# Gated product ahead of the scaling of o, and a cross attention that takes its four batches together

## The chip, the core and the metric

The kernel runs on one NeuronCore of a Trainium2 chip. Its engines are TensorE (PE in the rows, PEld for its weight loads), VectorE (DVE), ScalarE (ACT), GpSimd (POOL) and SyncE (SP), which here only issues transfers. Each engine runs its own instructions in the order of the program and waits on semaphores for the others. The metric is device time in microseconds (us), median of the runs; lower is better.

## The reference, cut to what matters

The input x is 4 batches of 512 tokens with 128 channels, the context 4 batches of 77 tokens. A cross attention is added to x through a gate, and then a stack of six layers of windowed attention and feed-forward.

```
xn = layernorm(x);  q = xn @ Wq.T + bq;  k, v = ctx @ Wk.T + bk, ctx @ Wv.T + bv
a  = softmax(q @ k.T / sqrt(128)) @ v
x  = x + tanh(g_xattn) * ((xn + a) @ Wo.T + bo)
y  = layernorm(x)
for i in range(6):                       # 16 heads of 64, windows of 32 tokens that look one window back
    y = attn(shift_tokens(y)) + y        # q and k with l2norm and rotary tables
    y = ffn(shift_tokens(y)) + y         # (a * gelu(gate)) @ W2 + b2, inner width 341
x  = x + tanh(g_ffn) * y
```

All data are float32.

## The kernel before

**The main loop.** The six layers are run as 192 units: a group is one layer of one batch (24 groups), and a group has 8 units (4 blocks of 128 tokens, two halves of the heads). One loop of 214 slots `n` is written out on each engine; `s = n % 8` is the place in the group. In slot n the engines work on several units at once: TensorE makes queries and keys of unit n, the scores of n-3, the product of probabilities and values (`attend`) of n-5, and so on. The feed-forward of group g-2 is spread over the slots by `s`. Its result is built in `uT`: TensorE's `up` products of the gate and of a, ScalarE's `gelu` on the gate, and VectorE's `gated(g, k)` (L942), which multiplies block k of a into it.

**Three PSUM banks in a ring.** Nearly every TensorE product of the loop goes to the next of three banks (`RING`), and waits until the result that stood there three turns ago has been read. In slot s = 3 the last turns are `up("gate", 1)`, `up("a", 0)`, `transpose_q`; in slot s = 4 the first are `attend` (L437), `values` (L378), `transpose_o` (L450). So `values` of s = 4 takes the bank of block 0 of a, and waits for `gated(g - 2, 0)`, which frees it.

**VectorE and GpSimd in a unit.** VectorE scales `o` by the inverse sum (`scale_o`, L884, reads the bank of `attend`), sums the next probabilities (L866), makes the inverse norms by a Newton step of three small instructions on 16 columns (`newton`, L823, L826, L828, two SBUF operands each), and scales k (L836) and q (L844). GpSimd then turns k and q by the rotary tables: L1033, L1040, L1076 for k, L1033, L1040, L1069 for q, all on SBUF.

**The cross attention** comes before the loop, in pairs of batches. The chain of a pair: statistics (L760, L763) on VectorE, inverse root on GpSimd (L1016, L1018), normalise (L769) on VectorE, transpose (L303), queries (L307), scores (L311), softmax on VectorE and ScalarE (L779 to L789, L590), transpose (L317), bias row (L321), attend (L326), transpose (L332), output projection (L337), the gated update of x (L800), again statistics and normalise (L760 to L769), transpose (L344) and copy to `xT` (L600, L601). The second pair uses the buffers and banks of the first, and so starts when the first is through. Ahead of both stand keys and values of the context (L289, L294, L295). GpSimd zeroes `kB` (L1008) first of all and multiplies the rotary tables (L1023) after the last inverse root.

Of the kernel before, what the change touches and what calls it, by code (L numbers as in the profile page):

```python
# [9 lines left out]
ALU = mybir.AluOpType  # L10
# [3 lines left out]
P = 128  # L14
B, N, C = 4, 512, 128
CTX = 77
# [50 lines left out]
def build(nc, x_in, ctx_in, g_xattn, g_ffn, Wq, bq, Wk, bk, Wv, bv, Wo_x, bo, Wqkv, q_scale, k_scale,  # L67
          Wo, ln_g, ln_b, W1, b1, W2, b2, rope_in, mats_in, mask_in, out):
    ctx = ExitStack()
    with ctx:  # L70
# [73 lines left out]
        xn_x = [quad(turned[:, j, 0, :]) for j in range(2)]  # L144
        xnT_x = [turned[:, j, 1, :] for j in range(2)]
        q_x = [turned[:, j, 2, :] for j in range(2)]
        res_x = [quad(turned[:, j, 3, :]) for j in range(2)]
        pr_x = [quad(qkn[:, j, 0:TPG * CTX], CTX) for j in range(2)]
        pT_x = [flat(pT[:, j]) for j in range(2)]
        rT_x = [flat(qT[:, j]) for j in range(2)]  # L150
        x_nat = oT[:, 0:B, :].rearrange("p b (t c) -> p (b t) c", c=C)
        small = lambda j, start, n: sq[:, 64 * j + start:64 * j + start + n]
        stats_x = [quad(small(j, 0, 6 * TPG), 6) for j in range(2)]
        mv_x = [quad(small(j, 24, 2 * TPG), 2) for j in range(2)]
        vare_x, rstd_x, mx_x, rs_x, rr_x = ([small(j, 32 + 4 * i, TPG) for j in range(2)] for i in range(5))
# [120 lines left out]
        def _(pe):  # L276
# [3 lines left out]
            for i in range(4):  # L280
                mm = pe.transpose(ps[0][:, i * C:(i + 1) * C], wx_in[:, i, :], ident[:, :])
            mm.then_inc(wxT_mm, 1)
            for b in range(B):
                mm = pe.transpose(ps[1][:, b * CTX:(b + 1) * CTX], ctx_sb[:, b, :], ident[0:CTX, 0:CTX])
            mm.then_inc(ctxT_mm, 1)
            pe.wait_ge(wxT_ev, 1)
            pe.wait_ge(ctxT_ev, 1)
            pe.wait_ge(cst_ready, 4)
            pe.matmul(ps[2][:, 0:B * CTX], wxT[:, 1, :], ctxT[:, :, :].rearrange("p b s -> p (b s)"),  # L289
                      start=True, stop=True).then_inc(kx_mm, 1)  # L290
# [6 lines left out]
            pe.wait_ge(kx_ev, 1)  # L297
            pe.wait_ge(vx_ev, 1)
            for pair in range(B // 2):
                for j in range(2):  # L300
                    pe.wait_ge(a_xn, 4 * (2 * pair + j) + 4)
                    for t in range(TPG):
                        mm = pe.transpose(ps[4 * j][:, t * P:(t + 1) * P], xn_x[j][:, t, :], ident[:, :])  # L303
                    mm.then_inc(a_xnT, 1)
                for j in range(2):
                    pe.wait_ge(a_xnTev, 2 * pair + j + 1)
                    pe.matmul(ps[4 * j + 1][:, :], wxT[:, 0, :], xnT_x[j], start=True, stop=True).then_inc(a_q, 1)  # L307
                for j in range(2):
                    pe.wait_ge(a_qev, 2 * pair + j + 1)
                    for t in range(TPG):  # L310
                        mm = pe.matmul(ps[4 * j + 2][:, t * P:t * P + CTX], q_x[j][:, t * P:(t + 1) * P],  # L311
                                       kxT[:, 2 * pair + j, :], start=True, stop=True)
                    mm.then_inc(a_sc, 1)
                for j in range(2):
                    pe.wait_ge(a_pn, 2 * pair + j + 1)
                    for t in range(TPG):
                        mm = pe.transpose(ps[4 * j + 3][0:CTX, t * P:(t + 1) * P], pr_x[j][:, t, :], ident[:, :])  # L317
                    mm.then_inc(a_pT, 1)
                for j in range(2):

                    pe.matmul(heads(ps[4 * j + 2][:, :], C), ones[0:1, :],  # L321
                              brow[0:1, 1, :].unsqueeze(1).to_broadcast([1, TPG, C]), start=True, stop=True)
                for j in range(2):
                    pe.wait_ge(a_pTev, 2 * pair + j + 1)
                    for t in range(TPG):
                        mm = pe.matmul(ps[4 * j][:, t * P:(t + 1) * P], pT_x[j][0:CTX, t * P:(t + 1) * P],  # L326
                                       vx[:, 2 * pair + j, :], start=True, stop=True)
                    mm.then_inc(a_att, 1)
                for j in range(2):
                    pe.wait_ge(a_res, 2 * pair + j + 1)  # L330
                    for t in range(TPG):
                        mm = pe.transpose(ps[4 * j + 1][:, t * P:(t + 1) * P], res_x[j][:, t, :], ident[:, :])  # L332
                    mm.then_inc(a_rT, 1)
                for j in range(2):
                    pe.wait_ge(a_rTev, 2 * pair + j + 1)
                    for t in range(TPG):
# [3 lines left out]
                for j in range(2):  # L340
                    b = 2 * pair + j
                    pe.wait_ge(b_x, 4 * b + 4)
                    for t in range(TPG):
                        mm = pe.transpose(ps[4 * j + 1][:, t * P:(t + 1) * P], x_nat[:, TPG * b + t, :], ident[:, :])  # L344
# [892 lines left out]
```

## Time and profile before

| | |
|---|---|
| median of 3 runs | 1879.38 us (1878.95 to 1880.2) |
| profiled execution, its own time | 1880.17 us |
| its span, first to last instruction | 1878.4 us |
| TensorE busy | 1770.3 us, 94% of the span |
| VectorE busy | 1610.7 us, 86% |
| GpSimd busy | 1499.3 us, 80% |
| ScalarE busy | 1326.8 us, 71% |
| cross attention and what is ahead of it | to 85.07 us, the first product of the loop |

A busy share is an average over the whole span, and a waiting instruction does not count as busy. Whether an engine that is busy for most of the time is also the one that sets the time is seen only from what it waited for, and from what the others waited for.

### The profile page before, as it was taken

Reading aid. Unit: us, or ns where it says so; the run is one execution under the profiler, and the core shown is the slowest. Engines: PE = TensorE matmul, PEld = TensorE weight load, DVE = VectorE, ACT = ScalarE, POOL = GpSimd, SP = SyncE. Lnnn points to the kernel's source line nnn. Section 1 sums busy time; section 2 is a strip of 40 time slices with the busy share of each in tenths; the row PEclk is TensorE's granted clock in tenths of the full one; section 3 lists DMA queues with packets and bytes.
Section 4 is the critical chain, followed back from the end, with each engine's and each line's share of the span. In section 5 each row is a group of like instructions: output and inputs, shape, how many; then the busy total and the mean of one; then the engine's idle time right before and its main releaser. Section 6 shows DMA issues by size and latency. Waiting matters only on the chain.

```text
span 1878.4 us, 48610 instructions
## 1 busy us (share of the span) xinstructions
PE 1770.3 (94%) x18100; PEld 1124.5 (60%) x18100; DVE 1610.7 (86%) x2780; ACT 1326.8 (71%) x2363; POOL 1499.3 (80%) x1200
## 2 busy tenths in 40 slices
PE   6689999999999999999999999999999999999986
PEld 4446655665666656666656666656666666566563
DVE  3499989989989899889899889898998998998873
ACT  2367777777777687777777777777777777877763
POOL 2299978888888888888888888888888888888760
PEclk8689999999999999999999999999999999999998
DMA  3013222223222223222222222222222222222221
GB/s 105 8 42 86 73 61 66 64 53 83 71 68 67 60 56 84 63 70 72 55 58 74 73 73 60 65 61 73 70 79 56 68 62 55 57 72 55 54 60 31
DMA packets 154989, 120.46 MB, mean 64 GB/s; under 512 B 42577, under 2 KB 151173, under 8 KB 154629
## 3 DMA queue, kind: packets, MB, share of 16 engines
q1 hardware_dynamic: 154757, 117.35, 24.2%
q8 instruction: 147, 2.41, 0.6%
q14 instruction: 85, 0.70, 0.1%
HBM read 18.66 MB, written 1.05 MB: 10 GB/s over the span
## 4 chain that ended last, share of the span: by engine, by line
PE 80%; DVE 9%; POOL 4%; issue 3%; SPq 1%; DMA 1%; ACT 1%; DVEq 0%; POOLq 0%; ACTq 0%
PE qk_bank L367 16%; PE ring_bank L437 10%; PE ring_bank L461 8%; PE ring_bank L378 8%; PE sc_bank L412 8%; PE ring_bank L505 7%; PE ring_bank L425 5%; PE ring_bank L388 4%; PE ring_bank L399 3%; PE ring_bank L450 3%; PE ring_bank L516 3%; POOL turned L1033 1%; POOL turned L1040 1%; DVE o L884 1%; DVE rn L828 1%
## 5 line engine op out<-in xcount | busy, mean ns | idle before, releaser
L1033 POOL TENSOR_TENSOR turned<-qkn,tables 128x512 f32<-128x512 f32 x384 | 489.7, 1275 | 230.4 <-DVE qkn L836 218.1
L1040 POOL TENSOR_TENSOR turned<-qkn,tables 128x512 f32<-128x512 f32 x384 | 499.2, 1300 | 0.0
L367 PE MATMUL qk_bank<-wqkv,xT 128*128 128x512 f32 x768 | 367.8, 602 | 6.9 <-DVE qkn L844 6.4
L619 ACT ACTIVATE vs<-ring_bank 128x512 f32<-128x512 f32 x192 | 114.6, 597 | 215.8 <-PE ring_bank L378 201.7
L1069 POOL TENSOR_TENSOR turned<-turned 128x512 f32<-128x512 f32 x192 | 254.0, 1323 | 15.0
L1076 POOL TENSOR_TENSOR turned<-turned 128x512 f32<-128x512 f32 x192 | 244.8, 1275 | 15.1
L378 PE MATMUL ring_bank<-wqkv,xT 128*128 128x512 f32 x384 | 216.5, 646 | 36.1 <-DVE uT L942 34.6
L437 PEld LDWEIGHTS ring_bank<-vw,pT 128*32 128x32 f32 x6144 | 156.8, 110 | 144.6 <-issue 144.5
L646 ACT ACTIVATE kB<-ring_bank 64x512 f32<-64x512 f32 x384 | 225.4, 587 | 23.2 <-PE ring_bank L399 20.9
L810 DVE TENSOR_REDUCE ss<-sq 128x16 f32<-128x1024 f32 x192 | 232.0, 1208 | 8.1 <-ACT sq L610 8.1
L884 DVE TENSOR_TENSOR o<-ring_bank,rr 128x512 f32<-128x512 f32 x192 | 132.3, 689 | 124.1 <-PE ring_bank L437 122.5
L437 PE MATMUL ring_bank<-vw,pT 128*32 128x128 f32 x6144 | 208.6, 277 | 0.1
L412 PE MATMUL sc_bank<-kB,qT 128*32 128x128 f32 x6144 | 207.5, 276 | 0.2
L610 ACT ACTIVATE sq<-qk_bank 128x1024 f32<-128x1024 f32 x192 | 198.3, 1033 | 0.0
L367 PEld LDWEIGHTS qk_bank<-wqkv,xT 128*128 128x128 f32 x768 | 132.2, 192 | 107.0 <-issue 93.8
L656 ACT ACTIVATE sc_bank<-mask_f 128x512 f32<-128x512 f32 x192 | 114.1, 594 | 106.5 <-DVE pr L859 106.5
L412 PEld LDWEIGHTS sc_bank<-kB,qT 128*32 128x32 f32 x6144 | 156.1, 109 | 34.2 <-issue 34.2
L461 PE MATMUL ring_bank<-oT,wo 128*128 128x256 f32 x768 | 173.8, 379 | 0.0
L450 PEld LDWEIGHTS ring_bank<-ident,o 128*128 128x128 f32 x768 | 95.5, 141 | 102.1 <-issue 94.3
L461 PEld LDWEIGHTS ring_bank<-oT,wo 128*128 128x128 f32 x768 | 142.2, 190 | 18.1 <-DVE uT L942 0.8
L505 PE MATMUL ring_bank<-xnT,w 128*128 128x512 f32 x288 | 142.2, 605 | 9.8 <-DVE xnT L933 7.7
L836 DVE TENSOR_TENSOR qkn<-qk_bank,rn 128x512 f32<-128x512 f32 x192 | 132.8, 692 | 20.7 <-DVE rn L828 0.9
(156 smaller groups left out, 3142.0 us busy)
## 6 DMA issues: line engine op xcount, KB each, us to landing
vw<-vs SPq DMA_DIRECT2D x1152, 64.0 KB, 2.1
vw<-vs SPq DMA_DIRECT2D x672, 32.0 KB, 1.9
wqkv<-in_L_ffn_Wqkv_dram SPq DMA_DIRECT2D x20, 384.0 KB, 3.5
wo<-in_L_ffn_Wo_dram SPq DMA_DIRECT2D x20, 128.0 KB, 3.3
w<-in_L_ffn_W_dram SPq DMA_DIRECT2D x6, 341.0 KB, 3.3
wqkv<-in_L_ffn_Wqkv_dram SPq DMA_DIRECT2D x1, 1536.0 KB, 10.2
x<-in_x_dram SPq DMA_DIRECT2D x2, 512.0 KB, 4.2
out_dram<-x SPq DMA_DIRECT2D x4, 256.0 KB, 2.3
```

The costliest lines, as they stand in the source:

```text
L367: mm = pe.matmul(QK[u % 2][:, i * UW:(i + 1) * UW], tok, wqkv[:, layer % 2, cut:cut + UW], start=True, stop=True)
L378: pe.matmul(RING[i % RINGS][:, :], xT[:, b, t * P:(t + 1) * P], wqkv[:, layer % 2, cut:cut + UW], start=True, stop=True).then_inc(ring_mad ...
L412: mm = pe.matmul(heads(SC_BANK[WIN * w:WIN * (w + 1), k * P:(k + 1) * P]), qT[:, u % 2, k, WIN * w:WIN * (w + 1)], kB[:, HP * half + k, :, ...
L437: mm = pe.matmul(heads(RING[i % RINGS][WIN * w:WIN * (w + 1), k * P:(k + 1) * P]), pT[:, u % 2, k, WIN * w:WIN * (w + 1)], vw[:, u % 2, w, ...
L461: mm = pe.matmul(RING[i % RINGS][:, 0:HALF], wo[:, layer % 2, k, :], oT[:, k, HALF * h:HALF * (h + 1)], start=(k == 0), stop=(k == KO - 1))
L505: pe.matmul(RING[i % RINGS][:, :], w1[:, DFF * j + k * P:DFF * j + (k + 1) * P], xnT[:, :], start=True, stop=True).then_inc(ring_made[i % ...
L646: ev = act.activation(kB[64 * h:64 * h + 64, HP * half:HP * half + HP, h, WIN + P * t:WIN + P * t + P], RING[i % RINGS][64 * h:64 * h + 64 ...
L810: dve.tensor_reduce(ss[:, :], heads(sq[:, :]), AX.X, ALU.add).then_inc(ss_done, 1)
L1033: return pool.tensor_tensor(heads(turned[:, u % 2, 2 * i, :]), heads(qkn[:, u % 2, i * UW:(i + 1) * UW]), table.unsqueeze(1).to_broadcast( ...
L1040: return pool.tensor_tensor(halves(turned[:, u % 2, 2 * i + 1, :]), halves(qkn[:, u % 2, i * UW:(i + 1) * UW])[:, :, ::-1, :], table.rearr ...
L1069: pool.tensor_tensor(q, q, turned[:, u % 2, 1, :], ALU.add).then_inc(q_summed, 1)
L1076: pool.tensor_tensor(k, k, turned[:, u % 2, 3, :], ALU.add).then_inc(k_summed, 1)
```

## The change

Two edits.

**1. Main loop, VectorE:** in slots with s = 4 `gated(g - 2, 0)` stands ahead of `scale_o(n - 5)`, where it stood behind it.

```diff
                 if s == 7:
                     add_attention(g - 1, 1)
+                if s == 4:
+                    gated(g - 2, 0)
                 scale_o(n - 5)
                 if s == 3:
                     layer_norm(g - 2)
-                if s == 4:
-                    gated(g - 2, 0)
```

**2. Cross attention:** the loop over pairs is gone. Each of the four batches has buffers of its own (in `oT`, `uT`, `dT` and `xnT`, which the main loop uses later) and two PSUM banks, and every engine does one step for all four batches and then the next step. The values of the context are made behind the scores, their copy on ScalarE stands ahead of the four exponentials, the bias row is written behind each transpose of the residual, and GpSimd's zeroing of `kB` stands between the inverse roots of the first and of the second normalisation.

```diff
-            for pair in range(B // 2):
-                for j in range(2):
-                    pe.wait_ge(a_xn, 4 * (2 * pair + j) + 4)
+            for b in range(B):
+                pe.wait_ge(a_xn, 4 * b + 4)
                     ...
+            for b in range(B):
+                pe.wait_ge(a_xnTev, b + 1)
+                pe.matmul(second_bank[b][:, :], wxT[:, 0, :], xnT_x[b], start=True, stop=True).then_inc(a_q, 1)
+            for b in range(B):
+                pe.wait_ge(a_qev, b + 1)
...
+                mm.then_inc(a_sc, 1)
             pe.wait_ge(small_dma, 16 * 6)
             for b in range(B):
-                o_ = ps[3][0:CTX, b * C:(b + 1) * C]
+                o_ = ps[7][0:CTX, b * C:(b + 1) * C]
...
+            act.activation(tg[:, :], gcol[:, :], ACT.Tanh).then_inc(tanh_ready, 1)
+            act.wait_ge(vx_mm, 1)
+            act.activation(vx[:, :, :].rearrange("p b c -> p (b c)"), ps[7][0:CTX, :], ACT.Copy).then_inc(vx_ev, 1)
+            for b in range(B):
+                act.wait_ge(a_sub, b + 1)
+                act.activation(pr_x[b], pr_x[b], ACT.Exp, scale=float(C) ** -0.5).then_inc(a_exp, 1)
...
+            for b in range(B + 1):
+                if b < B:
+                    dve.wait_ge(x_dma[b // 2], 16)
+                    statistics(b, row, a_stat)
+                if b > 0:
+                    normalise(b - 1, row, xn_x, a_stat, a_rstd, a_xn)
...
+            for b in range(B + 1):
+                if b < B:
                     rows = x1[:, TPG * b:TPG * (b + 1), :]
...
+                    statistics(b, row, b_stat)
+                if b > 0:
+                    normalise(b - 1, row, x_nat, b_stat, b_rstd, b_x)
...
+            inverse_roots(a_stat, a_rstd)
             pool.memset(kB[:, :, :, :], 0.0).then_inc(zero_ready, 1)
-            pool.wait_ge(cst_ready, 3)
...
+            inverse_roots(b_stat, b_rstd)
```

The order of the instructions at three places. VectorE in a slot with s = 4, before (L884 is `scale_o`, L942 `gated`, L866 `sum_p`, L823 the first step of `newton`):

```order
L859 TENSOR_TENSOR pr<-sc_bank,mx 128x512
L810 TENSOR_REDUCE ss<-sq 128x16
L816 TENSOR_TENSOR ssm<-ss,norm_min 128x16
L884 TENSOR_TENSOR o<-ring_bank,rr 128x512
L942 SCALAR_TENSOR_TENSOR uT<-ring_bank,b1f,uT 128x512
L866 TENSOR_REDUCE rs<-pr 128x8
L823 SCALAR_TENSOR_TENSOR step<-seed 128x16
```

and in the changed kernel (L888 is `scale_o`, L946 `gated`):

```order
L863 TENSOR_TENSOR pr<-sc_bank,mx 128x512
L814 TENSOR_REDUCE ss<-sq 128x16
L820 TENSOR_TENSOR ssm<-ss,norm_min 128x16
L946 SCALAR_TENSOR_TENSOR uT<-ring_bank,b1f,uT 128x512
L888 TENSOR_TENSOR o<-ring_bank,rr 128x512
L870 TENSOR_REDUCE rs<-pr 128x8
L827 SCALAR_TENSOR_TENSOR step<-seed 128x16
```

The gated product has moved past one instruction. GpSimd at the start of the program, before (L1016 and L1018 are the inverse root of one batch, its columns lie in `sq`):

```order
L1007 MEMSET w 128x43
L1008 MEMSET kB 128x8704
L1016 ISA
L1016 TENSOR_SCALAR sq<-sq 128x4
L1018 TENSOR_TENSOR sq<-sq,minus_half 128x4
```

and in the changed kernel (L1018 and L1020 are the inverse root, its columns lie in `xnT`), from the inverse root of batch 2 on:

```order
L1018 TENSOR_SCALAR xnT<-xnT 128x4
L1020 TENSOR_TENSOR xnT<-xnT,minus_half 128x4
L1018 TENSOR_SCALAR xnT<-xnT 128x4
L1020 TENSOR_TENSOR xnT<-xnT,minus_half 128x4
L1023 MEMSET kB 128x8704
L1018 TENSOR_SCALAR xnT<-xnT 128x4
```

The zeroing of `kB` now follows directly on the inverse root of the last batch. ScalarE in the changed kernel, from the queries' copies on (L589 copies the queries, L592 the values of the context, L595 is the exponential):

```order
L589 ACTIVATE uT<-qk_bank,bcol 128x512 x2
L589 ACTIVATE uT<-ring_bank,bcol 128x512
L589 ACTIVATE dT<-ring_bank,bcol 128x512
L590 ACTIVATE tg<-gcol 128x2
L592 ACTIVATE vw<-ring_bank 77x512
L595 ACTIVATE oT<-oT 128x308 x4
```

The exponentials stand behind the copy of the context's values, which stood ahead of everything of x before.

## Rows read from the trace of the kernel before

**Rows 1.** The page's chain that ended last, by engine.

```profile
PE 80%; DVE 9%; POOL 4%; issue 3%; SPq 1%; DMA 1%; ACT 1%; DVEq 0%; POOLq 0%; ACTq 0%
```

**Rows 2.** Waits of TensorE over the span: us in total, times, longest us.

```profile
PE ring_bank L378 <- DVE uT L942: 34.6, 22, 1.6
```

**Rows 3.** Timeline of VectorE from 950 us: start us, us, engine, line.

```profile
975.22 0.69 DVE L884 TENSOR_TENSOR o<-ring_bank,rr 128x512 f32<-128x512 f32 x1 [1.68 <-PE ring_bank L437]
975.83 0.74 DVE L942 SCALAR_TENSOR_TENSOR uT<-ring_bank,b1f,uT 128x512 f32<-128x512 f32 x1
...
984.41 0.69 DVE L884 TENSOR_TENSOR o<-ring_bank,rr 128x512 f32<-128x512 f32 x1 [0.55 <-PE ring_bank L437]
...
985.61 0.83 DVE L823 SCALAR_TENSOR_TENSOR step<-seed 128x16 f32<-128x16 f32 x1
...
986.97 0.69 DVE L836 TENSOR_TENSOR qkn<-qk_bank,rn 128x512 f32<-128x512 f32 x1
```

**Rows 4.** Timeline of TensorE in the same stretch.

```profile
976.62 1.13 PE L378 MATMUL ring_bank<-wqkv,xT 128*128 128x512 f32 x2 [1.57 <-DVE uT L942]
...
981.35 1.88 PE L367 MATMUL qk_bank<-wqkv,xT 128*128 128x512 f32 x4
...
1023.77 1.98 PE L367 MATMUL qk_bank<-wqkv,xT 128*128 128x512 f32 x4 [0.17 <-DVE qkn L844]
```

**Rows 5.** Timeline of GpSimd in the same stretch.

```profile
978.70 1.31 POOL L1033 TENSOR_TENSOR turned<-qkn,tables 128x512 f32<-128x512 f32 x1 [1.39 <-DVE qkn L836]
...
985.13 1.28 POOL L1069 TENSOR_TENSOR turned<-turned 128x512 f32<-128x512 f32 x1
...
1023.27 1.27 POOL L1033 TENSOR_TENSOR turned<-qkn,tables 128x512 f32<-128x512 f32 x1 [0.97 <-DVE qkn L836]
```

**Rows 6.** SyncE's timeline, and the landing times of `x` in its tile view.

```profile
7.04 0.43 SPq L1113 DMA_DIRECT2D x<-in_x_dram  x1
...
DMA to landing us min/median/max: 4.0/4.2/4.4
```

**Rows 7.** Timeline of TensorE in the cross attention.

```profile
10.94 0.71 PE L294 MATMUL qk_bank<-brow,ones 1*77 1x128 f32 x2
...
52.89 1.91 PE L307 MATMUL qk_bank<-turned,vw 128*128 128x512 f32 x2
...
56.30 1.06 PE L311 MATMUL qk_bank<-vw,turned 128*128 128x77 f32 x8
...
60.59 1.14 PE L317 MATMUL qk_bank<-ident,qkn 128*77 128x128 f32 x4 [2.19 <-DVE qkn L789]
...
66.47 2.08 PE L326 MATMUL qk_bank<-vw,pT 77*128 77x128 f32 x8
...
71.95 1.78 PE L337 MATMUL qk_bank<-vw,qT 128*128 128x128 f32 x8
...
82.46 1.11 PE L344 MATMUL ring_bank<-ident,oT 128*128 128x128 f32 x4 [1.89 <-DVE oT L769]
...
85.07 2.90 PE L367 MATMUL qk_bank<-wqkv,xT 128*128 128x512 f32 x4
```

**Rows 8.** Timeline of ScalarE in the cross attention.

```profile
16.14 0.59 ACT L578 ACTIVATE vw<-qk_bank 77x512 f32<-77x512 f32 x1 [4.58 <-PE qk_bank L295]
...
58.42 0.46 ACT L590 ACTIVATE qkn<-qkn 128x308 f32<-128x308 f32 x1 [1.19 <-DVE qkn L781]
```

**Rows 9.** Timeline of VectorE in the cross attention.

```profile
73.84 0.75 DVE L800 SCALAR_TENSOR_TENSOR x<-qk_bank,tg,x 128x512 f32<-128x512 f32 x1 [2.85 <-PE qk_bank L337]
...
78.28 1.11 DVE L769 TENSOR_SCALAR oT<-x,sq 128x128 f32<-128x128 f32 x4 [0.30 <-POOL sq L1018]
79.61 2.80 DVE L769 TENSOR_SCALAR oT<-x,sq 128x128 f32<-128x128 f32 x4 [0.21 <-POOL sq L1018]
```

**Rows 10.** Timeline of GpSimd in the cross attention.

```profile
0.88 7.35 POOL L1008 MEMSET kB<- 128x8704 f32 x1
...
79.54 2.77 POOL L1023 TENSOR_TENSOR tables<-rope,scales 128x256 f32<-128x256 f32 x4
```

More of the change, by code:

```diff
@@ new lines, in _ @@
+            for b in range(B):
+                pe.wait_ge(a_pn, b + 1)
+                if b == B - 1:
+                    pe.wait_ge(vx_ev, 1)
+                for t in range(TPG):
+                    mm = pe.transpose(second_bank[b][0:CTX, t * P:(t + 1) * P], pr_x[b][:, t, :], ident[:, :])
+                mm.then_inc(a_pT, 1)
+            for b in range(B):
+                pe.wait_ge(a_pTev, b + 1)
+                for t in range(TPG):
+                    mm = pe.matmul(first_bank[b][:, t * P:(t + 1) * P], pT_x[b][0:CTX, t * P:(t + 1) * P], vx[:, b, :],
+                                   start=True, stop=True)
+                mm.then_inc(a_att, 1)
@@ new lines, in _ @@
+            for b in range(B):
+                pe.wait_ge(a_res, b + 1)
+                for t in range(TPG):
+                    mm = pe.transpose(second_bank[b][:, t * P:(t + 1) * P], res_x[b][:, t, :], ident[:, :])
+                mm.then_inc(a_rT, 1)
+                pe.matmul(heads(first_bank[b][:, :], C), ones[0:1, :],
+                          brow[0:1, 1, :].unsqueeze(1).to_broadcast([1, TPG, C]), start=True, stop=True)
+            for b in range(B):
+                pe.wait_ge(a_rTev, b + 1)
+                for t in range(TPG):
+                    mm = pe.matmul(first_bank[b][:, t * P:(t + 1) * P], rT_x[b][:, t * P:(t + 1) * P], wxT[:, 3, :],
+                                   start=False, stop=True, skip_group_check=True)
+                mm.then_inc(a_y, 1)
@@ L346, in _ @@
+            for b in range(B):
+                pe.wait_ge(b_x, 4 * b + 4)
+                for t in range(TPG):
+                    mm = pe.transpose(second_bank[b][:, t * P:(t + 1) * P], x_nat[b][:, t, :], ident[:, :])
+                mm.then_inc(b_xT, 1)
             pe.matmul(SC_BANK[:, :], mean_w[:, :], rT_x[1], start=True, stop=True).then_inc(sc_open, 1)
@@ L375, in values @@
                 i = turn("v", u)
+                if u == 0:
+                    pe.wait_ge(xT_ready, 2 * B)
                 cut = 2 * INNER + half * UW
@@ new lines, in statistics, with normalise @@
+            def statistics(b, src, stat):
+                for t in range(TPG):
+                    dve.bn_stats(stats_x[b][:, t, :], src(b, t)).then_inc(stat, 1)
+                dve.wait_ge(stat, 2 * TPG * b + TPG)
+                for t in range(TPG):
+                    dve.bn_aggr(mv_x[b][:, t, :], stats_x[b][:, t, :]).then_inc(stat, 1)
+            def normalise(b, src, dst, stat, rst, done):
+                dve.wait_ge(rst, 2 * b + 2)
+                dve.wait_ge(stat, 2 * TPG * b + 2 * TPG)
+                for t in range(TPG):
+                    dve.tensor_scalar(dst[b][:, t, :], src(b, t), mv_x[b][:, t, 0:1], rstd_x[b][:, t:t + 1],
+                                      ALU.subtract, ALU.mult).then_inc(done, 1)
```

234 lines of the change are left out of this document (85 added, 149 removed).

## The prediction, made before the changed kernel ran

> **What bounds the kernel now.** I read the chain of waits on the page first: four fifths of it are TensorE, 9% VectorE, 4% GpSimd [rows 1]. Then TensorE's own waits: by far the largest repeated one is that of `values` (L378) for the gated product L942, 34.6 us in 22 waits, so 1.57 us in each group but the last two [rows 2]. The timelines of one group tell how it comes about. VectorE is idle for 1.68 us until `attend` is through, then scales o (L884, from 975.22), and only then makes the gated product (975.83 to 976.57) that frees the bank; TensorE, done with `attend` 1.57 us before 976.62, so at 975.05, stands still until then [rows 3, 4]. The cross attention is a stretch of its own: the loop's first product starts at 85.07 us [rows 7], and nothing in the loop can start before it.
>
> **Edit 1, the gated product first.** VectorE is free from 975.22 - 1.68 = 973.54 [rows 3]. The product takes 0.74 us and so ends at 974.3, before `attend` does (975.05); its other operands are older still. `values` then starts at 975.05. `scale_o` is not delayed, since it waits for `attend` anyway. Nothing is added, so this alone is worth the whole wait: 22 x 1.57 = 34.6 us, which is the ceiling of this edit.
>
> What is late next? I looked for the loop that doesn't pass through TensorE. From 978.70 to 1023.27 GpSimd starts five more units, 44.6 us, while TensorE runs the same five slots in 1023.77 - 981.35 = 42.4 us and has a wait for VectorE at the end of them (0.17 us) [rows 4, 5]. So in these five slots VectorE and GpSimd are the slower side, and the lead that they have at 981.35 is used up at 1023.77. What sets their pace is seen at 985.61: the first Newton step, an instruction on only 16 columns, takes 0.83 us, longer than the one on 512 columns ahead of it, and ends at 986.44, when GpSimd's sum of q ends (985.13 + 1.28 = 986.41) [rows 3, 5]. It reads two SBUF operands and is held until GpSimd's instruction is over. The scaling of k follows at 986.97, GpSimd's next unit behind that [rows 3]. In that form a unit costs 7.7 us of GpSimd work and 1.4 us of waiting.
>
> If TensorE is earlier by 1.57 us, `scale_o` of this slot starts at 984.41 - 1.57 = 982.84, and the first Newton step at 985.61 - 1.57 = 984.04, before GpSimd's last-but-one instruction ends (985.1). It is then released at 985.1, the second step slips in, and only the third is held until 986.41. From the end of the held step to L836 there are now 986.97 - 986.44 = 0.53 us, in which two more steps run; behind a held third step none runs, and I estimate that 0.1 of it is left: 0.43 us less in this unit. Unit by unit, three of the five have the long form now (the others already have the short one), and in one of them VectorE itself gets to `scale_o` so late that it may stay long. So the VectorE and GpSimd side gives 2 or 3 times 0.43, 0.85 to 1.3 us a group; TensorE takes the rest of its 1.57 us back as a longer wait for L844 at the end. Where the Newton step of the s = 4 slot isn't held, the 0.61 us that L942 took ahead of L866 [rows 3] is won on this side too, which raises it to the ceiling. I take 1.2 us, nearer to the upper of the two: **22 x 1.2 = 26 us**, between 19 (0.85) and 34.6 (1.57).
>
> **Edit 2, the four batches together.** I follow the chain of waits of the new order with the durations of the old steps.
> - The second half of x is issued at 7.04 and takes 4.4 us to land, so 11.44 [rows 6]. VectorE then needs statistics (1.2), normalise (1.1), statistics (1.2); the inverse root of batch 3 follows on GpSimd (1.45: the roots of two batches come 79.61 - 78.28 = 1.33 apart, and some 0.1 to pass between the engines), the last normalise (1.1) and transpose (1.1). The 1.2 is from L800 to L769, 78.28 - 73.84 = 4.44: two updates of 0.8, two statistics, 0.3 of waiting; 1.1 is L769 [rows 9]. That gives 18.6 for the first query product.
> - Queries: 56.30 - 52.89 = 3.41 for two batches, twice 6.8. Scores 4 x 1.06 = 4.2. Values of the context 16.14 - 10.94 = 5.2, which now lie in the chain, because the four exponentials stand behind their copy on ScalarE. From there to the first transposed probability: the copy 0.6 and 60.59 - 58.42 = 2.2 less the 0.4 for which VectorE was busy with the other batch, 2.4 [rows 7, 8].
> - Transposes and bias rows: 66.47 - 60.59 = 5.88 for two, 11.8. Attend and second transposes 71.95 - 66.47 = 5.48 for two, 11.0 [rows 7]. The output projection of the first batch then starts at 18.6 + 6.8 + 4.2 + 5.2 + 2.4 + 11.8 + 11.0 = 60.0.
> - 73.84 - 71.95 = 1.9 later VectorE takes over [rows 7, 9]. Its work per batch, 0.8 + 1.2 + 1.1 = 3.1, is more than TensorE's, so it sets the pace: 61.9 + 4 x 2.0 + 3 x 1.1 + 0.3 = 73.5. The last normalise runs beside the rotary tables as it does now, where it takes 2.80 in place of 1.11 us [rows 9, 10]: 76.3.
> - From there to the loop 85.07 - 82.46 = 2.6 [rows 7]: 79.0 against 85.07, a gain of 6 us.
>
> **The zeroing of kB** is the term that may take this back. It now starts on GpSimd at the moment at which batch 3 may be normalised (16.4 us by the sum above), and lasts 7.35 us [rows 10]. No row shows a normalise beside a zeroing. The lower bound is nothing. The upper one is the full 7.35: beside the tables each of the four normalise instructions took as long as one of GpSimd's four, 2.80 against 2.77 us, where alone they took 1.11 [rows 9, 10]. They wait for the end of a GpSimd instruction, and GpSimd's came first, at 79.54 against 79.61. The nearest row is that one, so I take the full price: L769 of batch 3 ends at 24.9 and TensorE, which has its transpose ahead of all queries, waits too. The loop starts at 86.3.
>
> The Trainium skill, "SBUF — State Buffer", section "SBUF: two separate sides", says that VectorE in a two-port mode and a GpSimd instruction share one pair of ports as a lock, held for a whole instruction, whether or not GpSimd reads; a zeroing would hold it for its whole length. The trace agrees for the tables and shows nothing on a zeroing; the rule would give the upper bound.
>
> **The clock.** The products of 128x512 took 1.91 us per pair of passes at L307 and 1.13 us at L378 (1.2 and 2.4 GHz) [rows 4, 7]; the sum above has TensorE at 1.2 GHz throughout. With twice as many products in one run the last two of the queries may come at 2.4 GHz, which saves 0.75 us each, 1.5 in all. That and the 1.3 us above cancel: **edit 2 is worth 0 us**, between a loss of 1.3 and, without the hold, a gain of 6 to 8 (up to 11, if the values run at 2.4 GHz too).
>
> **The sum.** 1880.2 (the profiled execution) - 26 - 0 = 1854; that execution is 0.8 us over the median shown, so I predict 1853.
>
> **Rivals.**
> - *The zeroing doesn't hold VectorE.* For it: nothing but that no row shows it; a zeroing reads nothing. Then edit 2 gives 6 to 8, and the time is 1853 - 7 = 1846. Chance 0.25.
> - *Edit 1 gives the whole wait.* For it: in the slots behind, VectorE mostly waits for `attend`. Against it: the 44.6 against 42.4 us. 1880.2 - 34.6 - 0.8 = 1845, or 1838 with the rival above. Chance 0.10.
> - *Edit 1 gives next to nothing, because the loop of VectorE and GpSimd sets the period already.* For it: its lead is gone at 1023.77. Against it: the short form of a unit, which TensorE's earlier `attend` makes possible. Left are 0 to 8 us of edit 2 and a few of edit 1: 1870 to 1879. Chance 0.10.
> - *Slower.* The gated product stands ahead of `scale_o` and delays it by 0.74 us in 24 groups, 17.8 us, with the new wait passed on to the Newton steps and to GpSimd, and with 1.3 us lost in edit 2: 1879.4 + 17.8 + 1.3 = 1898. This decides from the point at which VectorE no longer waits for `attend` in that slot; it is idle there for 1.68 us now, more than twice the 0.74 [rows 3]. Chance 0.03.
>
> **How the numbers follow.** The case of the forecast, with edit 1 between 19 and 34.6 and the zeroing held, has 0.5 and spans 1843 to 1861. With the first rival it reaches to 1838, and the range goes up to 1868 for a smaller share of edit 1. What is left out is most of the third rival and the fourth, and the lower tail of the two good cases together, under 0.2. A measurement of this kernel tells about 0.2%, 3.8 us, from no change: faster than 1875.6 is everything but the fourth rival and half of the third, and a rest for what I haven't seen: 0.91; within 0.2% 0.05; slower 0.04.
>
> **What would show it.** In the profile of the changed kernel: L383 (`values`) no longer waits for L946; TensorE's wait for the scaled q (L848) at L370 grows from 0.17 us a group to 0.3 to 0.7; GpSimd's waits of 1.4 us become 1.0 in some units; the period of a group falls by 0.9 to 1.6 us. VectorE's L771 of batch 3 lies across the zeroing L1023 and takes about 8 us; the first product of the loop, L370, starts near 85 us, or near 78 without the hold. VectorE's updates (L803) are one batch apart by 3.1 us. The prediction is wrong if L370 of the loop's start is off by more than 3 us from both, or if the group's period falls by under 0.8 us.

## The result: 24 us faster, by two parts that the prediction had weighted differently

| | before | after |
|---|---|---|
| median of the runs, us | 1879.2 (4 runs, 1878.9 to 1880.2) | **1855.0** (4 runs, 1851.2 to 1856.2) |
| profiled execution, us (span) | 1880.2 (1878.4) | 1855.3 (1853.5) |
| ratio after to before, 95% interval | | **0.9867** (0.985 to 0.9884) |
| first product of the loop, us from the start | 85.07 | 81.02 |
| from there to the last unit's first product, us | 1714.9 | 1693.5 |

The prediction was 1853.0 with a range of 1838 to 1868. The medians are 24.2 us apart. Of the 24.9 us between the two spans 4.05 lie ahead of the loop and 21.4 in it, less 0.5 behind it. The page of the changed kernel, its span, its busy times and its chain of waits, which answer to [rows 1]:

```profile
span 1853.5 us, 48613 instructions
PE 1770.5 (96%) x18100; PEld 1122.9 (61%) x18100; DVE 1621.2 (87%) x2780; ACT 1327.3 (72%) x2363; POOL 1497.1 (81%) x1200
...
PE 77%; DVE 11%; POOL 4%; issue 3%; SPq 2%; DMA 1%; ACT 1%; DVEq 0%; POOLq 0%; ACTq 0%
```

TensorE's waits (who waited for whom: us in total, times, longest):

```profile
PE qk_bank L370 <- DVE qkn L848: 16.8, 33, 3.2
...
PE ring_bank L393 <- POOL turned L1075: 11.1, 10, 2.8
...
PE ring_bank L293 <- DVE oT L771: 7.3, 1, 7.3
```

The wait of `values` for the gated product [rows 2] is gone. In its place stands a wait of the q and k product (L370) for the scaled q (L848), and a single one of 7.3 us in the cross attention.

**The loop.** The first product of each unit gives the length of a slot. One group of eight units, read as differences between such starts on TensorE's timeline (before from 1008.33, after from 993.85; slot 1 of the table is s = 0, so slot 5 is s = 4):

| slot | 1 | 2 | 3 | 4 | 5 | 6 | 7 | 8 | group |
|---|---|---|---|---|---|---|---|---|---|
| before | 7.55 | 7.89 | 10.26 | 10.44 | **9.19** | 7.55 | 10.15 | 9.28 | 72.31 |
| after | 7.55 | 8.08 | 10.25 | 10.43 | **7.56** | 8.21 | 10.25 | 9.27 | 71.60 |

Slot 5 lost the whole wait (1.63 us); slots 2 and 6 took back 0.85 of it, and slot 7 another 0.10. The rows of the after kernel around such a slot 6, first VectorE (the three Newton steps, the scaling of k, the scaling of q), then GpSimd, then TensorE:

```profile
970.37 1.12 DVE L827 SCALAR_TENSOR_TENSOR step<-seed 128x16 f32<-128x16 f32 x1
971.53 0.18 DVE L830 TENSOR_TENSOR step<-step,ssm 128x16 f32<-128x16 f32 x1
971.74 1.14 DVE L832 SCALAR_TENSOR_TENSOR rn<-step,seed 128x16 f32<-128x16 f32 x1
972.98 0.69 DVE L840 TENSOR_TENSOR qkn<-qk_bank,rn 128x512 f32<-128x512 f32 x1
973.59 0.68 DVE L848 TENSOR_TENSOR qkn<-qk_bank,rn 128x512 f32<-128x512 f32 x1
```

```profile
970.18 1.29 POOL L1046 TENSOR_TENSOR turned<-qkn,tables 128x512 f32<-128x512 f32 x1
971.54 1.30 POOL L1075 TENSOR_TENSOR turned<-turned 128x512 f32<-128x512 f32 x1
973.81 1.27 POOL L1039 TENSOR_TENSOR turned<-qkn,tables 128x512 f32<-128x512 f32 x1 [0.97 <-DVE qkn L840]
```

```profile
965.68 0.60 PE L393 MATMUL ring_bank<-ident,turned 128*128 128x128 f32 x4
966.11 1.88 PE L370 MATMUL qk_bank<-wqkv,xT 128*128 128x512 f32 x4
...
973.23 0.60 PE L393 MATMUL ring_bank<-ident,turned 128*128 128x128 f32 x4
974.32 1.13 PE L370 MATMUL qk_bank<-wqkv,xT 128*128 128x512 f32 x2 [0.49 <-DVE qkn L848]
```

The first step ends at 971.49, when GpSimd's L1046 ends (971.47); the second slips in; the third ends at 972.88, with L1075 (972.84). Two of the three steps of 0.17 us took 1.1 us each. The last fence also shows how a short wait is read: L393 and L370 start 0.43 us apart where nothing is waited for, and 1.09 apart at 973.23, so the wait is 0.66 us, of which the row shows 0.49. The modelled end of a product lies behind the point at which the next one can start, and by how much depends on the product: 0.17 us behind L393 here, but only 0.06 behind `attend` (the wait of 1.57 us at L378 was 1.63 in the slot). So a wait is longer than its row says by that much, and a shorter one is no idle time at all. The slot lengths show all of it.

**The cross attention.** TensorE, VectorE and GpSimd:

```profile
24.16 1.11 PE L293 MATMUL ring_bank<-ident,oT 128*128 128x128 f32 x4 [7.28 <-DVE oT L771]
25.06 3.16 PE L303 MATMUL qk_bank<-oT,vw 128*128 128x512 f32 x4
28.06 1.88 PE L303 MATMUL ring_bank<-oT,vw 128*128 128x512 f32 x4
29.77 1.91 PE L307 MATMUL qk_bank<-vw,uT 128*128 128x77 f32 x16
...
33.40 0.44 PE L313 MATMUL ring_bank<-brow,ones 1*77 1x128 f32 x2
...
35.99 0.44 PE L314 MATMUL ring_bank<-vw 128*77 128x128 f32 x2
38.70 2.25 PE L321 MATMUL qk_bank<-ident,oT 128*77 128x128 f32 x8 [2.26 <-DVE oT L793]
...
61.91 3.59 PE L339 MATMUL qk_bank<-vw,uT 128*128 128x128 f32 x16
...
81.02 1.63 PE L370 MATMUL qk_bank<-wqkv,xT 128*128 128x512 f32 x2
```

```profile
16.18 7.92 DVE L771 TENSOR_SCALAR oT<-x,xnT 128x128 f32<-128x128 f32 x4 [0.47 <-POOL xnT L1020]
```

```profile
16.10 7.35 POOL L1023 MEMSET kB<- 128x8704 f32 x1
```

Four normalise instructions that took 1.11 us before [rows 9] took 7.92 beside the zeroing. Behind that, the eight query passes took 4.7 us and the values of the context 2.9, where the prediction had 5.3 and 5.2. Each product row of the values is 0.44 us long here and was 0.71 before (L294, [rows 7]).

### The profile page after: what moved, and what is told of

It is laid out like the page before. It is cut to its first block, busy times and chain, and to the rows that moved or that the text cites. A ratio compares the mean times of both kernels' runs of the same rounds, so it can differ in the third digit from the quotient of the medians.

```text
span 1853.5 us, 48613 instructions
## 1 busy us (share of the span) xinstructions
PE 1770.5 (96%) x18100; PEld 1122.9 (61%) x18100; DVE 1621.2 (87%) x2780; ACT 1327.3 (72%) x2363; POOL 1497.1 (81%) x1200
## 4 chain that ended last, share of the span: by engine, by line
PE 77%; DVE 11%; POOL 4%; issue 3%; SPq 2%; DMA 1%; ACT 1%; DVEq 0%; POOLq 0%; ACTq 0%
PE qk_bank L370 17%; PE ring_bank L442 10%; PE ring_bank L466 9%; PE ring_bank L383 8%; PE sc_bank L417 7%; PE ring_bank L510 6%; PE ring_bank L430 4%; PE ring_bank L393 3%; PE ring_bank L455 3%; PE ring_bank L521 3%; PE ring_bank L404 3%; DVE rn L832 2%; DVE step L827 2%; DVE o L888 2%; POOL turned L1039 1%
## 5 line engine op out<-in xcount | busy, mean ns | idle before, releaser
L1046 POOL TENSOR_TENSOR turned<-qkn,tables 128x512 f32<-128x512 f32 x384 | 497.3, 1295 | 0.0
L370 PE MATMUL qk_bank<-wqkv,xT 128*128 128x512 f32 x768 | 368.7, 603 | 16.8 <-DVE qkn L848 16.8
L1075 POOL TENSOR_TENSOR turned<-turned 128x512 f32<-128x512 f32 x192 | 255.0, 1328 | 15.1
L888 DVE TENSOR_TENSOR o<-ring_bank,rr 128x512 f32<-128x512 f32 x192 | 132.0, 687 | 107.3 <-PE ring_bank L442 104.8
L370 PEld LDWEIGHTS qk_bank<-wqkv,xT 128*128 128x128 f32 x768 | 132.0, 192 | 120.5 <-issue 94.4
L466 PEld LDWEIGHTS ring_bank<-oT,wo 128*128 128x128 f32 x768 | 142.2, 190 | 18.1 <-DVE uT L946 0.8
```

The costliest lines, as they stand in the source:

```text
L370: mm = pe.matmul(QK[u % 2][:, i * UW:(i + 1) * UW], tok, wqkv[:, layer % 2, cut:cut + UW], start=True, stop=True)
L466: mm = pe.matmul(RING[i % RINGS][:, 0:HALF], wo[:, layer % 2, k, :], oT[:, k, HALF * h:HALF * (h + 1)], start=(k == 0), stop=(k == KO - 1))
L1046: return pool.tensor_tensor(halves(turned[:, u % 2, 2 * i + 1, :]), halves(qkn[:, u % 2, i * UW:(i + 1) * UW])[:, :, ::-1, :], table.rearr ...
L1075: pool.tensor_tensor(q, q, turned[:, u % 2, 1, :], ALU.add).then_inc(q_summed, 1)
```

## The experiments

Each is the kernel named with the edit shown; each was timed in three or more rounds against runs of the kernel before on the same chip (their median there 1879.7 to 1881.0, 1879.2 beside after). "After" is 1855.0; what a run is said to be under or over it is the difference of medians, and good to 2 us.

**1. The two edits apart.** First the gated product alone:

```diff
-                scale_o(n - 5)
-                if s == 3:
-                    layer_norm(g - 2)
                 if s == 4:
                     gated(g - 2, 0)
+                scale_o(n - 5)
+                if s == 3:
+                    layer_norm(g - 2)
```

> The kernel before with the gated product ahead of the scaling of o, and nothing else. Theory (a Newton step on VectorE is held by GpSimd's instruction, and that side gives only part of TensorE's 1.57 us a group): some 21 us faster than before, 1858 us, with TensorE's wait for the scaled q at some 13 us in place of 6.4. Rival (the two edits act on each other, for example the cross attention changes the phase in which the loop starts): less than 15 us or more than 27 us faster alone.

Measured: 1858.0 (1857.3 to 1859.4), ratio 0.9885 (0.987 to 0.99), 22.1 us faster. TensorE's wait for the scaled q came to 18.9 us, not 13. Then the changed kernel with this edit undone, that is, the cross attention alone:

> The changed kernel with the gated product back behind the scaling of o. Theory (edits add up): 4 us faster than before, 1875 us, the loop's first product at 81 us. Rival (the edits act on each other): no gain or a gain of over 8 us.

Measured: 1874.8 (1868.5 to 1877.0, six runs), ratio 0.9967 (0.9951 to 0.9983), 5.3 us faster. `values` waits for the gated product as before, 34.6 us in 22. So both parts count: the first is worth 22, the second 5, and together they gave 24, which is their sum within what these differences are good to.

**2. The zeroing of kB at the start again**, where `w1` is zeroed too:

```diff
             pool.memset(w1[:, 2 * DFF:], 0.0).then_inc(w1_pad, 1)
+            pool.memset(kB[:, :, :, :], 0.0).then_inc(zero_ready, 1)
...
             inverse_roots(a_stat, a_rstd)
-            pool.memset(kB[:, :, :, :], 0.0).then_inc(zero_ready, 1)
```

> The changed kernel with the zeroing of kB on GpSimd at the start of the program again, as the kernel before has it. Theory (the zeroing holds VectorE's normalise of batch 3 for its whole 7.35 us and TensorE waits behind it): the four instructions of that normalise take 1.1 us in place of 7.92, the loop starts 6 to 7.3 us earlier (74 to 75 us), 1848 us. Rival (the normalise is slow for another reason, or the first inverse roots now wait for the zeroing at the start and give it all back): the loop starts within 2 us of 81 us.

Measured: 1846.2 (1844.5 to 1847.3), ratio 0.982 (0.9806 to 0.9835), 8.8 us under after. The loop starts at 74.44, 6.6 us earlier, and TensorE's wait for batch 3 is 0.48 us in place of 7.28. The hold by the zeroing is real and costs about what it lasts. The Trainium skill, "SBUF — State Buffer", section "SBUF: two separate sides", calls the shared port pair a lock that is held for a whole instruction; the 7.92 us beside a zeroing of 7.35, and the 8.8 us gained by moving it, agree.

**3. One Newton step off VectorE.** ScalarE makes half the square of the seed, VectorE's first step goes, and the last one subtracts 1.5 in place of adding it:

```diff
+                act.wait_ge(seed_done, u + 1)
+                act.activation(halfsq[:, u % 2, :], seed[:, u % 2, :], ACT.Square, scale=0.5 ** 0.5).then_inc(half_done, 1)
...
-                dve.scalar_tensor_tensor(out=step[:, :], in0=sd, scalar=-0.5, in1=sd,
-                                         op0=ALU.mult, op1=ALU.mult).then_inc(newton_done, 1)
```

The sign of q and of k both turn, so the scores stay. In the changed kernel:

> The changed kernel with the first of the three Newton steps (half the square of the seed) made by ScalarE instead of VectorE; the sign of both q and k is turned by it, which leaves their product as it is. Theory (what is left of the 34.6 us is given back by VectorE's Newton steps being held by GpSimd): with one step less behind the sum of probabilities fewer units have a held last step, TensorE's wait for the scaled q falls from 16.8 us to under 8 us, and the kernel is 8 to 14 us faster than the changed one, 1841 to 1847 us. Rival (the rest was lost to ring banks that ScalarE empties late, or to TensorE itself): ScalarE has 0.25 us a unit more to do and the time is the same or up to 5 us longer.

Measured: **1817.9** (1814.2 to 1820.8), ratio 0.9664 (0.9647 to 0.9681). That is 37 us under after, more than twice the most that was expected. In the kernel before:

> The kernel before (gated product behind the scaling of o, cross attention as it was), with the first step of the reciprocal root (x -0.5 of the seed's square, 0.17 to 1.2 us of VectorE a unit) taken over by a Square on ScalarE. Theory: the 1.57 us a group that TensorE waits for uT come from the order, since VectorE itself stands idle for 1.68 us ahead of L884 and only then reaches the gated product; a shorter VectorE chain leaves that wait whole, and only slots 2 to 4 of a group (7.89, 10.26 and 10.44 us against 7.55, 10.15 and 10.20 with the Square) give back about 0.65 x 22 = 14 us: 1866 (1860 to 1870), with L378<-L946's like still at 34 in 22. Rival: the two edits add up, and the Square is worth here what it was behind the change, 31 to 37 us: 1843 to 1849, with the wait for uT cut to less than half.

Measured: 1862.8 (1862.2 to 1862.9), ratio 0.9905 (0.9888 to 0.9921), 18.1 us faster. Its largest wait of TensorE:

```profile
PE ring_bank L380 <- DVE uT L943: 34.6, 22, 1.6
```

The slots, from 1008.33 (before), 993.85 (after), 998.99 (Square in before) and 976.72 (Square in after), tell how the two edits work together:

| slot | 1 | 2 | 3 | 4 | 5 | 6 | 7 | 8 | group |
|---|---|---|---|---|---|---|---|---|---|
| before | 7.55 | 7.89 | 10.26 | 10.44 | 9.19 | 7.55 | 10.15 | 9.28 | 72.31 |
| gated first (after) | 7.55 | 8.08 | 10.25 | 10.43 | 7.56 | 8.21 | 10.25 | 9.27 | 71.60 |
| Square in before | 7.55 | 7.56 | 10.15 | 10.20 | 9.19 | 7.56 | 10.15 | 9.27 | 71.63 |
| both | 7.56 | 7.55 | 10.15 | 10.20 | 7.55 | 7.56 | 10.14 | 9.28 | 69.99 |

The order costs 1.63 in slot 5 and nothing else. The length of VectorE's chain costs 0.33 in slot 2 before and 0.53 after, 0.65 in slot 6 but only after, and 0.1 to 0.24 in slots 3, 4 and 7. Slot 5's wait was also VectorE's rest: without it the chain's length shows in slot 6. Only with both does TensorE have no wait in the rows of this group, 70.0 us of its own work, and then 2.3 us a group are gone, against 0.7 and 0.7 one by one. Of the 37 us, 31.3 lie in the loop (1693.5 to 1662.3) and 3.6 behind the last unit's first product (78.9 to 75.3), where the clock plays a part (experiment 7).

**4. Is it VectorE's chain, or ScalarE's new instruction?** The Square added, with VectorE left as it is:

> The changed kernel with the Square on ScalarE added and VectorE's chain left as it is (the Square's result is unused). Theory: the gain of the Square came from VectorE's shorter chain alone, and ScalarE has room for 0.2 us more a unit: 1855 (1852 to 1859). Rival: the small ScalarE instruction itself shifts something: more than 4 us either way.

Measured: 1853.7 (1851.5 to 1855.0), ratio 0.9858 (0.9844 to 0.9873). No change against after. The gain of experiment 3 came from VectorE's shorter chain.

**5. More small instructions, to find what one costs.** In the changed kernel, ahead of the first step, one or two copies of it with an unused result:

```diff
                 dve.wait_ge(seed_done, u + 1)
+                dve.scalar_tensor_tensor(out=spare[:, 0, :], in0=sd, scalar=-0.5, in1=sd,
+                                         op0=ALU.mult, op1=ALU.mult)
```

> The changed kernel with one more small VectorE instruction a unit, a copy of the first step of the reciprocal root (two inputs of 128x16 from SBUF) ahead of it, its result unused. Theory: a small instruction is held until GpSimd's instruction ends and the next one then slips through, so three steps meet two ends, and four meet the same two: the chain grows by the 0.2 us of the instruction alone, in the two slots of a group without slack: 0.4 x 22 = 9, so 1864 (1859 to 1872), and group periods of 72.0 against 71.6. Rival: each such instruction costs what the one taken away gave back (37 us): 1892. Rival: VectorE's length does not matter and the gain came from elsewhere: 1855.

Measured: 1899.7 (1891.5 to 1901.2), ratio 1.0093 (1.0068 to 1.0117): 44.7 us slower than after, not 9.

> The changed kernel with two more such instructions a unit, five in a row. Theory: a third end of a GpSimd instruction is met, 1.3 us on top of 2 x 0.2: the two slots without slack grow by about 1.4, the two with 0.6 to 0.7 us of slack by 0.7 to 0.8: 4 us a group, 1855 + 22 x 4 = 1943 (1910 to 1955), that is far more than twice what one instruction costs. Rival (each instruction the same): 1855 + 2 x what one more cost, 1873 if that was 9, 1929 if it was 37.

Measured: 1927.7 (1919.0 to 1928.1), ratio 1.0239 (1.0215 to 1.0264): the second costs 28 more. My count of GpSimd's ends was wrong twice. Of the eight chains of a group, two that meet one end in after meet two with four steps, which I had not counted; with five steps a third end is met in one of the eight, where I had reckoned with it in four. So the same place, with a kind of instruction that isn't held:

```diff
                 dve.wait_ge(seed_done, u + 1)
+                dve.reciprocal(spare[:, :], sd)
```

> The changed kernel with one more small VectorE instruction a unit at the same place as the one that cost 44.7 us, but of a kind that no row shows held beside GpSimd: a reciprocal of the 128x16 seed (the reciprocals of the profile take 0.19 us, all of them), result unused. Theory: the cost was that of one more instruction that can be held; this one only lengthens the chain by 0.2 us, most of it taken up in the wait for the same end of GpSimd's instruction: 1860 (1855 to 1868). Rival: the cost was the 0.2 us of length, that moves the chain past GpSimd's next start: 1890 to 1901 as with the other.

Measured: 1890.2 (1881.2 to 1893.0, eight runs), ratio 1.0051 (1.0037 to 1.0064): 35 us for 0.24 us a unit. The theory that the number of instructions that can be held decides is dead: length alone gives 35 of the 44.7, and the kind of the instruction at most the other 9.5. How, the rows show of the chain that VectorE starts some 20 us behind the group's first product. In after (group from 993.85), then with the reciprocal (group from 1014.78), and TensorE of the latter in slot 4:

```profile
1013.98 0.16 DVE L827 SCALAR_TENSOR_TENSOR step<-seed 128x16 f32<-128x16 f32 x1
1014.17 1.16 DVE L830 TENSOR_TENSOR step<-step,ssm 128x16 f32<-128x16 f32 x1
1015.36 0.17 DVE L832 SCALAR_TENSOR_TENSOR rn<-step,seed 128x16 f32<-128x16 f32 x1
```

```profile
1035.08 0.24 DVE L828 RECIPROCAL spare<-seed 128x16 f32<-128x16 f32 x1
1035.23 1.20 DVE L829 SCALAR_TENSOR_TENSOR step<-seed 128x16 f32<-128x16 f32 x1
1036.47 0.17 DVE L832 TENSOR_TENSOR step<-step,ssm 128x16 f32<-128x16 f32 x1
1036.68 1.14 DVE L834 SCALAR_TENSOR_TENSOR rn<-step,seed 128x16 f32<-128x16 f32 x1
```

```profile
1046.87 0.66 PE L431 MATMUL ring_bank<-ident,pr 128*128 128x128 f32 x4 [0.63 <-DVE o L890]
1047.92 1.96 PE L511 MATMUL ring_bank<-xnT,w 128*128 128x512 f32 x4 [0.39 <-DVE xnT L939]
```

In after this chain meets one end of GpSimd's instructions, in 18 of the 19 groups in the middle; with the reciprocal it meets two, in all 19. It starts 0.17 us later in the group (20.30 for 20.13), and k is scaled 1.35 us later (23.14 for 21.79). Slot 4, with the normalise of the layer norm in it, follows without a wait of VectorE, and TensorE now waits there for two of VectorE's results: 11.46 us where after has 10.43. That is 1.0 us a group, and slots 2 and 6 add 0.3: together 1.3 (72.9 against 71.6), 29 us in 22 groups. The loop as a whole is 34.0 us longer, 5.2 of them in its second group alone. The three small steps and the reciprocal, grouped by line, show how the work grows (busy us in all 192 units, mean ns of one). After, then the kernel with the reciprocal:

```profile
L827 DVE SCALAR_TENSOR_TENSOR step<-seed 128x16 f32<-128x16 f32 x192 | 113.0, 588 | 1.9 <-ACT seed L632 1.9
...
L830 DVE TENSOR_TENSOR step<-step,ssm 128x16 f32<-128x16 f32 x192 | 91.8, 478 | 6.6
...
L832 DVE SCALAR_TENSOR_TENSOR rn<-step,seed 128x16 f32<-128x16 f32 x192 | 76.0, 396 | 6.6
```

```profile
L829 DVE SCALAR_TENSOR_TENSOR step<-seed 128x16 f32<-128x16 f32 x192 | 159.1, 829 | 0.0
L834 DVE SCALAR_TENSOR_TENSOR rn<-step,seed 128x16 f32<-128x16 f32 x192 | 128.7, 670 | 6.6
...
L832 DVE TENSOR_TENSOR step<-step,ssm 128x16 f32<-128x16 f32 x192 | 54.5, 284 | 6.6
L828 DVE RECIPROCAL spare<-seed 128x16 f32<-128x16 f32 x192 | 46.2, 240 | 1.9 <-ACT seed L633 1.9
```

The steps sum to 281 us after and to 388 with the reciprocal: 46 us of new work made 108: the chain above and the one some 58 us into the group each have two held steps where after has one. With one step less the sum was 162, 119 us less for 0.17 us a unit of own work. Why a chain of given length falls into one form or the other in each slot I can read but did not manage to forecast.

**6. The cross attention's wait, and the clock.** ScalarE's four exponentials ahead of its copy of the context's values:

```diff
-            act.wait_ge(vx_mm, 1)
-            act.activation(vx[:, :, :].rearrange("p b c -> p (b c)"), ps[7][0:CTX, :], ACT.Copy).then_inc(vx_ev, 1)
             for b in range(B):
                 act.wait_ge(a_sub, b + 1)
                 act.activation(pr_x[b], pr_x[b], ACT.Exp, scale=float(C) ** -0.5).then_inc(a_exp, 1)
+            act.wait_ge(vx_mm, 1)
+            act.activation(vx[:, :, :].rearrange("p b c -> p (b c)"), ps[7][0:CTX, :], ACT.Copy).then_inc(vx_ev, 1)
```

> The changed kernel with ScalarE's four exponentials (L595) placed ahead of its copy of the context's values (L592). Theory: they start as soon as each batch's scores are there, TensorE no longer stands idle for 2.26 us ahead of L321 at 38.70, and because it doesn't, its granted clock stays at full speed through the next stretch, as with the three edits together (no idle at 29.04, full clock until 40): 2 us of wait plus 6 to 9 us of products that run at 2.4 instead of 1.2 GHz, so 1845 (1843 to 1849) and the loop's first product near 71. Rival: the clock falls when it will, and only the wait goes: 1853, first product near 79.

Measured: 1843.7 (1842.8 to 1844.6, three runs; a fourth took 6402 us and is not counted), ratio 0.9807 (0.979 to 0.9823), 11.3 us under after. The loop starts at 70.17, and the granted clock stays at full speed until 48 us. Then the same idle time filled in another way, with products that serve nothing:

```diff
             mm.then_inc(vx_mm, 1)
+            for i in range(5):
+                pe.matmul(second_bank[0][:, :], wxT[:, 0, :], wxT[:, :, :].rearrange("p a c -> p (a c)"),
+                          start=True, stop=True)
```

> The changed kernel with five products of 128x512 more in the cross attention, behind the context's values (L314), into a bank that nobody reads then: they fill TensorE's idle 2.26 us ahead of L321 and do nothing else. Theory: the granted clock fell there because TensorE stood idle; kept busy it stays at full speed, and the 27 us of products behind it get shorter by 6 to 9 us: 1848 (1845 to 1851) although work was added, loop start near 73. Rival: the fall has nothing to do with the idle: 1855, loop start 81.

Measured: 1846.6 (1845.4 to 1850.4), ratio 0.982 (0.9804 to 0.9836): **8.4 us under after, with work added**; the slowest of its four runs is under the fastest of after's (1851.2). The granted clock (the third last column) by stretches, after and then this kernel; the columns ahead of it are the length of the stretch and the busy us of TensorE, its weight loads, VectorE, ScalarE and GpSimd, with the number of instructions in brackets:

```profile
38.00:40.00 2.00, 1.30 (x5) 0.96 (x6) 1.90 (x6) 0.59 (x3) 0.00 (x0) 0.50 0.00 0
...
44.00:46.00 2.00, 2.00 (x12) 2.00 (x11) 0.69 (x1) 0.00 (x0) 0.00 (x0) 0.50 0.00 0
...
54.00:58.00 4.00, 4.00 (x8) 1.53 (x8) 0.00 (x0) 1.12 (x2) 0.00 (x0) 0.50 0.00 0
```

```profile
38.00:40.00 2.00, 2.00 (x5) 1.12 (x5) 0.33 (x1) 1.31 (x4) 0.00 (x0) 0.50 0.00 0
...
44.00:46.00 2.00, 2.00 (x20) 2.00 (x19) 0.19 (x1) 1.41 (x3) 0.00 (x0) 1.00 0.00 0
...
54.00:58.00 4.00, 4.00 (x12) 2.08 (x12) 0.00 (x0) 0.60 (x1) 0.00 (x0) 0.57 0.00 0
```

After is at 1.2 GHz from 37.8, within its idle time, to 65.2. The filled kernel is at 1.2 GHz from 37.5, in the midst of products, and back at 2.4 from 41 to 54.5. Its TensorE rows:

```profile
37.37 0.65 PE L313 MATMUL ring_bank<-brow,ones 1*77 1x128 f32 x2
37.95 0.71 PE L314 MATMUL ring_bank<-vw 128*77 128x128 f32 x2
38.45 5.66 PE L317 MATMUL qk_bank<-vw 128*128 128x512 f32 x10
43.95 1.04 PE L324 MATMUL qk_bank<-ident,oT 128*77 128x128 f32 x8
```

So my reason does not hold. The clock did not fall because TensorE stood idle: here it fell at nearly the same time (0.44 to 0.65 us at L313) while TensorE was busy. What differs is the return to full speed, and the idle time alone does not decide that either. The profiled execution of the cross attention alone (experiment 1) has the same wait of 2.26 us ahead of L321, fell at 37.9 and was back at 44.7:

```profile
44.00:46.00 2.00, 2.00 (x17) 2.00 (x16) 0.79 (x2) 0.00 (x0) 0.00 (x0) 0.82 0.00 0
```

Shown is the gain: both ways of taking the idle time out are faster than after in every counted run, and the mean granted clock of the span is 0.987 to 0.990 in all of these runs against 0.981 to 0.986 in after's four. By what way the idle time acts on the clock is not shown. The fillers ran partly at the low clock and delayed L324 by 5 us, and the products behind them made up more than that.

**7. Three edits together**: the Square, the zeroing at the start, the exponentials first.

> The changed kernel with three edits together: the Square on ScalarE, the zeroing of kB at the start again, and in the cross attention ScalarE's four exponentials ahead of the copy of the context's values. Theory: the first two touch different stretches and add, 1817.9 - 8.8 = 1809; the third brings the transposes of the products (L321) forward by the 0.6 us of the copy: 1808.5 (1805 to 1812). Rival: with the loop bound by TensorE alone the earlier start is eaten somewhere in it: 1815 or more.

Measured: **1805.3** (1804.6 to 1807.7), ratio **0.9602** (0.9588 to 0.9616), 50 us under after and 75 under before, at the low end of what was expected. Its loop starts at 63.11 and takes 1662.8, as with the Square alone. The exponentials did not only bring L321 forward by the 0.6 us of the copy: TensorE has no wait ahead of it (two of 0.45 us follow within the transposes), and the full clock lasts until 40 us. From L321 to L339 it takes 15.0 us, where after takes 23.2. Against the Square alone the loop starts 18.4 us earlier and the profiled time is 15.3 less; 2.5 of the difference were lost behind the last unit (77.8 us from its first product to the end, 75.3 with the Square alone). I made no experiment on it, but the granted clock differs there: in the 6 us that begin 18 us behind that product it is 0.50 in this kernel and in after, and 1.00 with the Square alone.

## Why the prediction was right, and where it was not

- **Edit 1 takes the wait away whole, and VectorE and GpSimd take a part of it back** ("TensorE takes the rest of its 1.57 us back as a longer wait for L844 at the end"): right, shown by the slots and by experiment 1. Slot 5 lost 1.63, slots 2, 6 and 7 took 0.95.
- **The size, 1.2 us a group and 26 in all**: measured 22.1 as a time by itself. In the loop of after the 22 groups in the middle gave 17.9, 0.81 each (0.90 each with edit 1 alone), and the last 1.7. The first gave 1.8 more, but that is not edit 1's: edit 1 alone gave nothing there and edit 2 alone 2.3. The mis-sized term is "2 or 3 times 0.43": it came out at just under two, below the middle that I took for the chance that the whole would be won. The step behind it was right in kind: in the chain of slot 6 the first Newton step alone was held before, and in after the first and the third are, as the rows from 970.37 show. GpSimd's waits of 1.4 us fell from 84 to 66 and those of 1.0 rose from 25 to 41.
- **"The VectorE and GpSimd side"** as the limit: right in that a shorter VectorE chain frees it (experiment 3), incomplete in its price. I had VectorE's own length as cover ("in the slots behind, VectorE mostly waits for `attend`"). The doses of experiment 5 show how thin that cover is: 0.24 us a unit cost 35 us.
- **The zeroing of kB holds VectorE for its full length**: right, 7.92 us, and 8.8 us back when it is moved. Rival 1 is out.
- **Edit 2 is worth 0**: wrong, it is 5.3 by itself, and in after 4.05 up to the start of the loop (81.02 for 85.07) and 1.8 in its first group. The failed step is the clock: "two of the query products at 2.4 GHz", 5.3 us for the queries, and 5.2 for the values with TensorE at 1.2 GHz. The rows have 4.7 and 2.9, and the scores 3.6 for 4.2. The product rows of the values are 0.44 us long in place of 0.71; of the same kind, L314 in the filled kernel took 0.71 at a granted clock of 0.50. The step to L321 held, 2.35 for 2.4. The held normalise let the queries begin 0.8 earlier than summed (25.06 for 25.9). From L321 on the sum held too: 23.2 for 22.8, 2.2 for 1.9, 14.3 for 14.4, 2.62 for 2.6. The prediction had this case in its bounds ("if the values run at 2.4 GHz too") and did not give it its share.
- Two errors of opposite sign, 4 to 6 too much in edit 1 and 4 to 6 too little in edit 2, gave a time that was off by 2 us. That closeness is luck: the sum was better than its terms.
- **What would show it**: `values` no longer waits: yes. L370's wait 0.3 to 0.7 a group: 16.8 us in 33 waits, of 0.35 to 0.5 us mostly, and 0.17 us more for each that the rows don't show. The group's period falls by 0.9 to 1.6: no, by 0.71 in the group shown and 0.81 on average, at the 0.8 that I had set as the mark of a wrong step. The updates L803 3.1 apart: 3.0. L370 near 85 or 78: 81.02, off by more than the 3 us that I had set from both, and there was a wrong step.
- **Slower** was not near: ahead of `scale_o` VectorE still waits for `attend` in 106 of the 192 units, 104.8 us in all.

## What to carry to other kernels

Where a tuned loop has two limits that cover each other, taking away one shows little (0.7 us a group each way here) and both show all (2.3): price a second edit in the kernel that has the first. Read the length of a repeated slot between the starts of the same instruction, not the idle time, which misses 0.06 to 0.17 us of each wait here and the short waits altogether. And in a stretch where the clock comes and goes, time the kernel without a short idle: the 2.3 us ahead of 27 us of products were worth 11.3 us here when taken out and 8.4 when filled.

## What the runs showed of the hardware that I had not expected

- Useless products made the kernel faster: five more of 128x512 in an idle of 2.26 us, 8.4 us less in all.
- Unbroken work did not bring the full clock back: in after TensorE has no idle time in its rows from 38.70 us on, and the granted clock stays at 0.50 until 65.2.
- The granted clock's column can say 1.00 where the products are at the low speed: in the kernel before it says so from 10.9 to 16 us, while L294 took 0.71 us. Ahead of the first recorded fall, go by the length of the products.
- The granted clock of a short stretch differs between executions of one kernel. With the cross attention alone, the profiled execution, the fastest of its six, was back at full clock at 44.7 us (eight products of L326 in 1.06 us, 1.91 in after) and started the loop at 75.23, 5.8 us ahead of after on the same program part; its six runs spread over 8.5 us, those of the kernel before over 3.3.
- A VectorE instruction of 128x16 that costs 0.17 us took 1.1 to 1.2 beside a GpSimd product of 128x512, up to the end of it, in up to two of the three steps of a chain; the reciprocals of 128x8 and the reductions from SBUF never did (0.19 and 1.21 us in each of 192 units).
- GpSimd's products were slowed in turn: beside VectorE's two-operand work of 128x512 (L928, L930) two of them took 1.71 and 1.61 us in place of 1.27.
